# State-space audio tower: the scan's two states side by side, one more turned pair, and work moved between VectorE and GpSimd

## The reference

```
h = tokens @ W + b                               # 128 wide
z = layernorm(h)
for direction in (forward, backward):            # Mamba block, 256 channels, 16 states
    xi, gate = split(z @ in_proj)
    xc = silu(causal_conv4(xi))
    dt, B, C = split(xc @ x_proj)
    delta = softplus(dt @ dt_w + dt_b)
    for t: state = exp(delta * A) * state + delta * xc * B     # 256 x 16 states
           y = sum over states of state * C
    out += (y + xc * D) * silu(gate) @ out_proj
q = layernorm(out / 2 + z);  h1 = h + q * ln_g + ln_b
result = h1 + layernorm(h1)
```

## Time and profile before

| | |
|---|---|
| median of 3 runs | 3269.98 us (3268.59 to 3270.75) |
| profiled execution, its own time | 3269.01 us |
| its span | 3267.2 us |
| granted clock of TensorE | 0.971 of full |
| time up to the first scan | 59.3 us |
| product with C on GpSimd, x1024 | 2346.3 us busy, 225.1 us idle before it |
| scan on VectorE, x1024 | 2270.3 us busy, 127.7 us idle before it |

### The profile page before, as it was taken

How to read it: one execution, slowest core, us unless ns; L and a number is a source line. 1 busy time by engine, 2 the same in 40 slices (tenths; PEclk the granted TensorE clock), 3 DMA queues, 4 the chain that set the end, 5 groups by cost and what they waited for, 6 DMA issues and landing times.

```text
span 3267.2 us, 53223 instructions
## 1 busy us (share of the span) xinstructions
PE 2929.2 (90%) x18304; PEld 2225.0 (68%) x18304; DVE 3031.7 (93%) x2455; ACT 3006.6 (92%) x5633; POOL 2943.1 (90%) x1829
## 2 busy tenths in 40 slices
PE   5899898999899998999999999999989988999985
PEld 3776766776767766667667677677667666676664
DVE  4999999999999999999999999999999999999995
ACT  4999999999999999999999999999999999999994
POOL 2889999999999999999999999999999999999996
PEclk9999999999999999999999999999999999999997
DMA  2223222232322232222222222322222322222221
GB/s 76 94 83 95 93 90 87 81 97 93 96 91 88 80 97 91 91 92 84 95 91 92 90 91 83 97 91 92 91 91 83 97 91 91 91 82 94 90 87 45
DMA packets 102208, 290.53 MB, mean 89 GB/s; under 512 B 11371, under 2 KB 36150, under 8 KB 101942
## 3 DMA queue, kind: packets, MB, share of 16 engines
q1 hardware_dynamic: 101942, 287.12, 27.7%
HBM read 276.84 MB, written 10.24 MB: 88 GB/s over the span
## 4 chain that ended last, share of the span: by engine, by line
PE 42%; ACT 23%; DVE 12%; POOL 11%; issue 11%; SPq 0%; DVEq 0%; DMA 0%; POOLq 0%; ACTq 0%
PE y_ps L331 13%; POOL hc L819 9%; ACT da L677 8%; PE m_ps L364 6%; ACT w L623 6%; DVE hc L931 6%; PE g_ps L331 6%; PE m_ps L373 4%; PE m_ps L426 4%; DVE g_ps L918 3%; ACT L664 3%; PE m_ps L380 2%; PE m_ps L387 2%; PE g_ps L450 2%; PE g_ps L451 2%
## 5 line engine op out<-in xcount | busy, mean ns | idle before, releaser
L819 POOL TENSOR_TENSOR hc<-hc,c_all 128x1000 f32<-128x1000 f32 x1024 | 2346.3, 2311 | 225.1 <-DVE hc L931 210.7
L931 DVE TENSOR_TENSOR_SCAN hc<-da,g_ps 128x1012 f32<-128x1012 f32 x1024 | 2270.3, 2250 | 127.7 <-PE g_ps L331 58.1
L677 ACT ACTIVATE da<-delta,a_neg 128x498 f32<-128x498 f32 x2048 | 1330.9, 698 | 5.8 <-DVE hc L931 5.0
L331 PEld LDWEIGHTS y_ps<-ident,hc 128*125 128x125 f32 x8192 | 1044.0, 194 | 299.4 <-issue 183.3
L331 PE MATMUL y_ps<-ident,hc 128*125 128x128 f32 x8192 | 1115.2, 281 | 42.1 <-POOL hc L819 42.0
L623 ACT ACTIVATE w<-ut,bt 125x256 f32<-125x256 f32 x2048 | 891.8, 496 | 0.5
L331 PE MATMUL g_ps<-ident,w 125*128 125x125 f32 x4096 | 569.6, 285 | 226.1 <-DVE hc L931 219.3
L331 PEld LDWEIGHTS g_ps<-ident,w 125*128 125x128 f32 x4096 | 467.1, 147 | 277.0 <-DVE hc L931 264.5
L918 DVE TENSOR_TENSOR g_ps<-u,g_ps 128x1000 f32<-128x1000 f32 x512 | 608.5, 1188 | 42.7 <-PE g_ps L451 42.0
L364 PE MATMUL m_ps<-zt,convw 128*128 128x500 f32 x1024 | 473.3, 584 | 0.7 <-ACT zt L560 0.7
L364 PEld LDWEIGHTS m_ps<-zt,convw 128*128 128x128 f32 x1024 | 189.0, 190 | 151.8 <-issue 120.7
(11 more groups left out here) (59 smaller groups left out, 2133.6 us busy)
## 6 DMA issues: line engine op xcount, KB each, us to landing
c_all<-c_rows SPq DMA_DIRECT2D x512, 500.0 KB, 3.6
xin<-x_t SPq DMA_DIRECT2D x32, 375.0 KB, 7.6
out<-out_sb SPq DMA_DIRECT2D x32, 250.0 KB
c_rows<-dbl SPq DMA_DIRECT2D x64, 31.2 KB, 1.6
c_all<-f_conv_w SPq DMA_DIRECT2D x1, 512.0 KB
c_all<-b_conv_w SPq DMA_DIRECT2D x1, 512.0 KB
hc<-f_in_w SPq DMA_DIRECT2D x1, 128.0 KB
inw<-f_in_w SPq DMA_DIRECT2D x1, 128.0 KB
```

The source lines that it names most:

```text
L331: return pe.matmul(dst, src, ident[0:rows, 0:rows], start=first, stop=last, is_transpose=True, skip_group_check=True)
L677: op = act.activation(states(da[n % RING])[j].rearrange("p (s t) -> p s t", s=SC)[:, :, 1:T], steps, ACT.Exp, scale=a_neg[:, p % 2, db, 2 ...
L819: pool.tensor_tensor(hc, hc, c_all[:, pair % CRING], ALU.mult).then_inc(hc_ready, 1)
L931: dve.tensor_tensor_scan(h[n % HRING][:, 0:UC], da[n % RING][:], g_ps[n % 2][:, 0:UC], 0.0, ALU.mult, ALU.add).then_inc(scanned, 1)
```

## The change

It does five things. The two states lie end to end, in `da` and `h` at 0 to 1000 and in `g_ps` at columns 12 to 1012 (LEAD = BANK - TC), so that the first state ends where the first bank ends; the scan runs over 1000 columns. Pair 3 is made by ScalarE in place of pair 4, at steps 0 to 2. Pair 5 is turned too, made by GpSimd at steps 2 and 4 of the phase. -mean and variance + eps are made by VectorE right behind the statistics, after a wait for the aggregate. The turn of z, both halves of the out-projection and the norm of z are issued at other steps.

```diff
-UC = BANK + TC
+LEAD = BANK - TC
-TURN, TAIL0, TAIL1, TOKENS = (0, 11), (0, 13), (0, 15), (1, 15)
-STATS_Z, POW_Z, NORM_Z = (0, 1), (0, 3), (0, 7)
+TURN, TAIL0, TAIL1, TOKENS = (0, 13), (0, 15), (1, 4), (1, 15)
+STATS_Z, POW_Z, NORM_Z = (0, 1), (0, 3), (0, 8)
-W_ACT = {2: [(-2, 4), (-1, 4)], 4: [(0, 2), (1, 2), (2, 2), (3, 2)], 6: [(6, 3), (7, 2), (8, 3)], 7: [(9, 3), (10, 3), (11, 2)]}
-W_POOL = {}
+W_ACT = {2: [(-2, 4), (-1, 4)], 3: [(0, 3), (1, 3), (2, 2)], 6: [(6, 3), (7, 2), (8, 3)], 7: [(9, 3), (10, 3), (11, 2)]}
+W_POOL = {5: [(2, 1), (4, 1)]}
...
-        da = [sb(f"da{j}", [128, UC]) for j in range(RING)]
-        h = [sb(f"hc{j}", [128, 2 * BANK]) for j in range(HRING)]
+        da = [sb(f"da{j}", [128, 2 * TC]) for j in range(RING)]
+        h = [sb(f"hc{j}", [128, 2 * TC]) for j in range(HRING)]
...
-            return tile[:, 0:TC], tile[:, BANK:UC]
+            return tile[:, 0:TC], tile[:, TC:2 * TC]
+        def across(g):
+            return g[:, LEAD:LEAD + 2 * TC]
...
-                            at = e * BANK + j * TP
+                            at = LEAD + e * TC + j * TP
...
-                    pe.matmul(g[:, 0:TC], pick[:, 2 * r, :], upper(dbl[p % 2][0:K2, :]), start=True, stop=True)
-                    pe.matmul(g[:, BANK:UC], pick[:, 2 * r + 1, :], upper(dbl[p % 2][0:K2, :]),
+                    pe.matmul(g[:, LEAD:BANK], pick[:, 2 * r, :], upper(dbl[p % 2][0:K2, :]), start=True, stop=True)
+                    pe.matmul(g[:, BANK:BANK + TC], pick[:, 2 * r + 1, :], upper(dbl[p % 2][0:K2, :]),
...
-                pool.wait_ge(ln_step[n], 2 * c + 2)
-                pool.tensor_scalar(minus_mean[:, n, :], meanvar[:, n, :, 0], -1.0, None, ALU.mult)
-                pool.tensor_scalar(vareps[:, n, :], meanvar[:, n, :, 1], EPS, None, ALU.add).then_inc(ln_pow[n], 1)
-                pool.wait_ge(ln_pow[n], 2 * c + 1)
+                pool.wait_ge(ln_step[n], 3 * c + 3)
                 pool.tensor_tensor(rstd[:, n, :], vareps[:, n, :], half[:], ALU.pow).then_inc(ln_pow[n], 1)
...
-                hc = paired(h[n % HRING])
-                pool.tensor_tensor(hc, hc, c_all[:, pair % CRING], ALU.mult).then_inc(hc_ready, 1)
+                hc = h[n % HRING][:]
+                pool.tensor_tensor(hc, hc, c_all[:, pair % CRING].rearrange("p n t -> p (n t)"), ALU.mult).then_inc(hc_ready, 1)
...
-            for j in range(2):
-                dve.memset(g_ps[j][:, TC:BANK], 0.0).then_inc(setup_dve, 1)
...
-                dve.wait_ge(ln_step[n], 2 * c + 1)
+                dve.wait_ge(ln_step[n], 3 * c + 1)
                 for j in range(NT):
                     op = dve.bn_aggr(meanvar[:, n, j, :], stats[:, n, j, :])
                 op.then_inc(ln_step[n], 1)
+                dve.wait_ge(ln_step[n], 3 * c + 2)
+                dve.tensor_scalar(minus_mean[:, n, :], meanvar[:, n, :, 0], -1.0, None, ALU.mult)
+                dve.tensor_scalar(vareps[:, n, :], meanvar[:, n, :, 1], EPS, None, ALU.add).then_inc(ln_step[n], 1)
...
-                g = paired(g_ps[n % 2])
+                g = across(g_ps[n % 2]).rearrange("p (n t) -> p n t", n=2)
...
-                dve.tensor_tensor_scan(h[n % HRING][:, 0:UC], da[n % RING][:], g_ps[n % 2][:, 0:UC], 0.0,
+                dve.tensor_tensor_scan(h[n % HRING][:], da[n % RING][:], across(g_ps[n % 2]), 0.0,
```

More of the change, by code:

```diff
@@ L245, in audio_tower_kernel @@
         LOADED = 16 * len(loads)
-        SETUP_DVE = 1 + RING + 2 + 1 + 1 + 2 * TAPS + 1 + 4
+        SETUP_DVE = 1 + RING + 1 + 1 + 2 * TAPS + 1 + 4
         def states(tile):
-            return tile[:, 0:TC], tile[:, BANK:UC]
+            return tile[:, 0:TC], tile[:, TC:2 * TC]
+        def across(g):
+            return g[:, LEAD:LEAD + 2 * TC]
         def upper(tile):
             return tile.bitcast(BF16).rearrange("p (t two) -> p t two", two=2)[:, :, 1]
-        def paired(tile):
-            return tile[:, 0:2 * BANK].rearrange("p (n t) -> p n t", n=2)[:, :, 0:TC]
         def wait_drained(eng, *j):
@@ L764, in power @@
             def power(n, c):
-                pool.wait_ge(ln_step[n], 2 * c + 2)
-                pool.tensor_scalar(minus_mean[:, n, :], meanvar[:, n, :, 0], -1.0, None, ALU.mult)
-                pool.tensor_scalar(vareps[:, n, :], meanvar[:, n, :, 1], EPS, None, ALU.add).then_inc(ln_pow[n], 1)
-                pool.wait_ge(ln_pow[n], 2 * c + 1)
+                pool.wait_ge(ln_step[n], 3 * c + 3)
                 pool.tensor_tensor(rstd[:, n, :], vareps[:, n, :], half[:], ALU.pow).then_inc(ln_pow[n], 1)
-                pool.wait_ge(ln_pow[n], 2 * c + 2)
+                pool.wait_ge(ln_pow[n], c + 1)
                 if n == 2:
```

## The result

| | before | after |
|---|---|---|
| median | 3270.36 us (4 runs) | 3483.82 us (3481.3 to 3484.06, 4 runs) |
| ratio | | 1.065, 95% interval 1.0635 to 1.0665 |
| profiled execution, its span | 3269.01, 3267.2 us | 3481.3, 3479.5 us |
| granted clock | 0.971 | 0.963 |

The change costs 213 us, 6.5%. The forecast was 3311, with 3350 at the upper end: the sign came out, the size was wrong by a factor of five, and the engine that I had named as the bound was another.

What follows compares the result with a forecast made beforehand. The prediction took VectorE as the bound before and GpSimd after: 93.2 + 9.3 - 1.8 = 100.7 us a chunk against 99.3, +42 over 31 chunks, -3 first, +2 last, giving 3311 us; range for 8 in 10: 3205 to 3350.

Steps and rivals of the forecast that it cites:

- The norm's small operations: Minus_mean and variance + eps moved from GpSimd to VectorE: GpSimd -1.8 us a chunk, VectorE +1.3.
- VectorE's stall: VectorE's waits, 2.5 us a chunk in the kernel before; taken out of its demand of 96.8 us, summed to 92.0 after.
- The rival: VectorE's small operations wait for GpSimd's running one: 10.4 us a chunk, VectorE 102.4, time 3365 or about 3345; chance 0.12.
- TensorE at 92.3 hides its work: TensorE trades two products for eight transposes per newly turned pair: +1.4 us a chunk, to 92.3, under GpSimd's 100.7.
- The place of pair 3: ScalarE makes pair 3 for pair 4 at steps 0 to 2: cost 0, since it fills three units ahead.
- GpSimd bound at 100.7: GpSimd's sum per chunk, 93.2 + 9.3 - 1.8 = 100.7 us, becomes the bound, above the present period of 99.3.
- GpSimd's backlog covers the others' bursts: Five h buffers let GpSimd lag about four units, 9 us; waits for scans of several microseconds a chunk would refute it.
- The w operation at 2.33: Pair 5's operations on GpSimd, 1024 columns each: 2.33 us, four a chunk, +9.3; from below 1.88, from above 3.0.
- Turned pairs, -5.3 on VectorE: One more turned pair per phase, four steps a chunk at 2.16 us instead of 3.49: VectorE saves 5.3 us.
- The scan, -0.85: VectorE's scan goes from 1012 to 1000 columns, 32 x 27 ns: -0.85 us a chunk.
- The chunk's steps: Out-projection halves and turn of z at other steps: no charge; could take the 1.7 us hole at (0,15) from VectorE.
- The forecast's case: GpSimd bound at the two-input price: 3311 us, own range 3290 to 3335, chance 0.45.

Runs made afterwards that it cites:

- a2: Changed kernel, small operations still on VectorE but -1 and eps read from a per-partition column in SBUF instead of given in the instruction: 3572.6 us.
- a1: Changed kernel with the norm's two small operations given back to GpSimd: 3293.68 us, ratio 1.0071 to the kernel before.
- a3: Changed kernel with pair 4 turned by ScalarE as before instead of pair 3, GpSimd's pair 5 kept: 3412.94 us.
- A: Letter for the layout part, the states end to end; alone on the kernel before: 3260.47 us.
- D: Letter for the chunk's steps (turn of z, out-projections, norm of z); alone on the kernel before: 3300.3 us.
- d1: Kernel before with the states end to end and the later chunk steps, tables and small operations as before: 3283.24 us, ratio 1.0038.
- C: Letter for the norm's small operations moved to VectorE; alone on the kernel before: 3424.56 us.
- B: Letter for the tables, pair 3 for 4 on ScalarE and pair 5 on GpSimd; the changed kernel without them: 3447.98 us.
- c4: Changed kernel with the norm's two small operations on ScalarE instead of VectorE: 3410.23 us, ratio 1.0426 to the kernel before.
- b1: Kernel before with the states end to end alone, scan over 1000 columns: 3260.47 us, ratio 0.997.
- b4: Kernel before with the chunk's steps alone moved (turn of z, out-projections, norm of z): 3300.3 us, ratio 1.0091.

## Why the prediction was wrong

**The norm's small operations** are the step that failed, and they decided the case. I took six at 0.15 plus three waits, +1.3 us a chunk, from the 188 ns of the earlier trace rows, a row with GpSimd idle. They measure 965 and 1036 ns, 6.0 us a chunk. With them 3483.82, without 3293.68. Moving them was to spare GpSimd 1.8 us a chunk; it cost 190 us of time. The hold alone would not have done it in my own sum: VectorE at 92.0 - 1.3 + 6.0 = 96.7 lies under GpSimd's 100.7. The second failed term is VectorE's stall, which I counted at nothing: 9.2 us a chunk.

**The rival named this mechanism and priced it wrongly.** It had the hold at 10.4 us a chunk and VectorE at 102.4; the hold is 6.0 and the period 106.2. It left out VectorE's waits for TensorE. My demand without the small operations was 92.0 - 1.3 = 90.7 and counted no stall; 90.7 + 6.0 of small operations + 9.2 of waits is 105.9. I had 0.12 on it, since the trace spoke neither way; and my range ended at 3350, under the 3365 that the rival itself gave. A wait that no row of the trace could rule out, on the engine that was the bound, deserved more.

The Trainium skill, page "SBUF — State Buffer", section "Who interferes with whom", holds that a tensor_scalar in the two-port mode and a GpSimd operation exclude each other for the whole instruction. For the immediate form, started inside a GpSimd operation, the trace agrees, 24 to 30 ns from end to end; that these operations run in the two-port mode, no run shows. It does not agree in every case: the 41 vareps of 157 ns lie beside a GpSimd operation, and neither is held in the records. For the pointer form, a2 measures it held as well, at 1200 and 1748 ns.

**TensorE at 92.3 hides its work** failed as an argument on sums. The sum is nearly right (93.75 in a1). But five turned pairs need a fill each at steps where side jobs already fill TensorE: 19.5 us of 19.9. VectorE's waits rose from 2.7 to 9.2 us a chunk. The place of pair 3, which I costed at nothing since ScalarE works three units ahead, is 71 us of the time by a3, about two thirds of it waits: I looked for the price on ScalarE, and it came on TensorE. The rest of these waits isn't divided further.

**GpSimd bound at 100.7** is wrong for the change: VectorE sets the pace there. That a1 measures 100.14 is luck in part, since two errors cancel: the w operations were priced 1.7 us a chunk too high, and a1 does not have the 1.8 us of relief. The claim that GpSimd's backlog covers the others' bursts holds in a1 (9 us of waits for scans in all). By the sign that I set for it, waits of several microseconds a chunk, it fails in after: GpSimd waits 7.8 us a chunk, as VectorE is slower than it.

**The w operation at 2.33**: 1.90. My lower bound, 1.88 from the rows with a 2-byte input, was the one to take; the standing input is cheaper than a plain one. The row that I predicted at 2.36 is wrong by 0.46; against the 2.33 of the sum that is 1.7 us a chunk on GpSimd.

**Turned pairs, -5.3 on VectorE**: four products less, 455.1 us for 608.5, 4.8 us a chunk busy. In time, beside A and D, the tables bring a loss: d1 3283.24, a1 3293.68. VectorE's busy time does fall, but GpSimd is full in a1, and VectorE waits instead.

**The scan, -0.85**: -0.8, of which 0.3 arrives in the period.

**The chunk's steps, "I charge nothing"**: 30 us alone, 23 us with the layout, nothing in the whole. The reason was wrong too: with the second half moved, the hole stayed. The late fill stands behind the first half, and at the new place the product of (1,6) waits longer, 2.23 us.

**The forecast's case** is seen in a1, which is not the change: GpSimd bound, 3293.68, within the likeliest case's own range and 17 us under its 3311. The sign of the change came out by another cause than the forecast had. The kernel would have been slower without C too, by 24 us. In order the parts read A -10, D +23, B +10, C +190; of other orders, C alone +154, D last -1.5. They don't add.

## What to carry to other kernels

Before a small operation goes to VectorE beside a busy GpSimd, price it at the other engine's running instruction: 3 x 2 operations a chunk over four columns cost 190 us here, and at their old place 2 us of GpSimd a chunk. An engine's sum over a chunk hides nothing that is wanted at a given step; look at the fullest stretch of each engine and ask which step waits in it. And take each part alone before the whole: the layout was worth 10 us by itself, and everything else hid it.

## What the hardware showed that I had not expected

- A VectorE tensor_scalar over four columns that starts inside a GpSimd operation is held to its end in both forms (means of minus_mean: immediate 965 ns, pointer 1200 ns; 155 to 230 ns where an operation is not held). One that starts as the next GpSimd operation starts was held in 52 of 93 cases in the immediate form (after), in 93 of 93 in the pointer form (a2). Beside the same GpSimd, bn_stats (278 ns), bn_aggr (157 ns), product (1185 ns) and scan (2228 ns) are not.
- On ScalarE the same two take 198 and 285 ns in c4, not held: about two thirds of them start inside a GpSimd operation, and the longest of all takes 302 ns.
- A GpSimd product of f32 with an input that stands still along the row takes 1903 ns for 1024 columns, where a plain one takes 2316 for 1000.
- The time that TensorE's records show at the lower clock was 190 us before, 257 after, 159 in a1, 255 in b1 and 292 in b4. b1 is faster than before with more of it, a1 slower with less. What share of a time is due to it stays open, but it can't be the cause of the 213 us: in the kernel before, eight transposes took 1.92 us at a granted clock of 0.51 and 1.04 at 0.99, so the 67 us more of it after than before are worth at most about 34 (an estimate, as if TensorE had set the pace in all of them).
